# VectorE's up product directly behind the weighting, ahead of attention and routing, in a two-layer kernel

## What is computed

```python
q, k, v = ...                                  # three 128x128 projections of xn
attn = softmax(einsum('nqd,nkd->nqk', q, k) * HD ** -0.5)
x_att = (attn @ v) @ out_w.T + out_b           # 16 heads of 8; the 8 batches attend to each other at one sequence position

scores = sigmoid(xn @ w_gate.T)                # 16 experts in 4 groups: best 2 groups, best 4 experts
combine = normalised scores of the chosen experts, 0 elsewhere
g = silu(einsum('th,efh->tef', xn, w1_e));  u = einsum('th,efh->tef', xn, w3_e)
routed = einsum('tef,ehf,te->th', g * u, w2_e, combine)
shared = (silu(xn @ w1_s.T) * (xn @ w3_s.T)) @ w2_s.T
out = x + x_att + routed + shared
```

## Time and profile before

| | before |
|---|---|
| time, median of 3 runs | 355.44 us (355.14 to 356.28) |
| the profiled execution's own time | 355.92 us |
| its span, first to last instruction | 354.1 us |
| VectorE (DVE) busy | 311.0 us, 88% of the span |
| TensorE (PE) busy | 304.5 us, 86% |
| GpSimd (POOL) busy | 250.2 us, 71% |
| ScalarE (ACT) busy | 178.9 us, 51% |
| TensorE's granted clock, mean | 0.979 of full speed |

### The profile page before, as it was taken

How to read it: one execution, slowest core, us unless ns; L and a number is a source line. 1 busy time by engine, 2 the same in 40 slices (tenths; PEclk the granted TensorE clock), 3 DMA queues, 4 the chain that set the end, 5 groups by cost and what they waited for, 6 DMA issues and landing times.

```text
span 354.1 us, 5666 instructions
## 1 busy us (share of the span) xinstructions
PE 304.5 (86%) x1771; PEld 252.0 (71%) x1771; DVE 311.0 (88%) x826; ACT 178.9 (51%) x499; POOL 250.2 (71%) x162
## 2 busy tenths in 40 slices
PE   0568877899898987589999999899998999989995
PEld 0246555777686776477877887698987888878785
DVE  4995899979879677976999999899998999989795
ACT  3345766778786767677242531613516235162520
POOL 4184667826557361117999899989999899988671
PEclk9996999999999999879999999999999999999999
DMA  5590000000000000004853332423424334253102
GB/s 142 161 302 9 2 0 1 2 1 1 3 0 3 0 0 3 0 4 122 182 128 93 102 105 90 118 61 91 149 82 111 120 94 115 59 148 114 38 2 59
DMA packets 21321, 24.91 MB, mean 70 GB/s; under 512 B 2420, under 2 KB 12060, under 8 KB 21292
## 3 DMA queue, kind: packets, MB, share of 16 engines
q1 hardware_dynamic: 20248, 24.09, 24.7%
q10 hardware_dynamic: 820, 0.39, 0.4%
q0 software_dynamic: 224, 0.08, 0.1%
HBM read 22.19 MB, written 2.36 MB: 69 GB/s over the span
## 4 chain that ended last, share of the span: by engine, by line
DVE 37%; PE 34%; POOL 12%; issue 10%; ACT 6%; DMA 1%; DVEq 0%; POOLq 0%; ACTq 0%
PE Q L944 16%; PE VN L944 8%; PE T L944 7%; POOL prod_qk L874 6%; POOL prod_pv L884 4%; DVE hid L1632 4%; DVE rope_b L1368 3%; DVE rope_a L1366 3%; DVE att L1591 2%; PE T L940 2%; DVE sgc L1619 2%; DVE scr L1577 2%; DVE bst L1209 2%; DVE attn L1398 2%; DVE xT_lo L1419 1%
## 5 line engine op out<-in xcount | busy, mean ns | idle before, releaser
L874 POOL TENSOR_TENSOR prod_qk<-qkv 128x1024 f32<-128x1024 f32 x32 | 76.6, 2412 | 2.9 <-DVE above L1461 2.1
L884 POOL TENSOR_TENSOR prod_pv<-prob,qkv 128x1024 f32<-128x1024 f32 x32 | 69.0, 2195 | 7.4 <-DVE att L1591 5.1
L773 ACT ACTIVATE Q<-Q 128x512 f32<-128x512 f32 x48 | 27.5, 581 | 56.5 <-PE Q L944 56.3
L1632 DVE TENSOR_TENSOR hid<-T,sgc 128x512 f32<-128x512 f32 x64 | 43.4, 679 | 0.1
L944 PE MATMUL Q<-bias,ones 128*128 128x400 f32 (+1 forms) x64 | 30.3, 474 | 15.2 <-ACT v_ext L663 7.1
L1577 DVE TENSOR_REDUCE scr<-prod_qk 128x128 f32<-128x1024 f32 x32 | 38.8, 1211 | 5.0 <-POOL prod_qk L874 5.0
L944 PEld LDWEIGHTS Q<-w,hid 128*128 128x128 f32 x288 | 37.5, 191 | 3.4 <-DVE hid L1632 0.6
L944 PEld LDWEIGHTS VN<-w,hid 128*128 128x128 f32 x288 | 37.6, 191 | 3.1
L944 PE MATMUL Q<-w,hid 128*128 128x128 f32 x288 | 38.0, 275 | 0.4 <-DVE hid L1632 0.4
L944 PE MATMUL T<-xT_hi,w_hi 128*128 128x512 f32 x72 | 31.2, 434 | 8.2 <-DVE hid L1632 7.9
L1591 DVE TENSOR_REDUCE att<-prod_pv 128x128 f32<-128x1024 f32 x32 | 38.2, 1195 | 0.0
(11 more groups left out here) (186 smaller groups left out, 801.1 us busy)
## 6 DMA issues: line engine op xcount, KB each, us to landing
cw<-comb_table SPq DMA_DIRECT2D x62, 256.0 KB, 4.6
out_x<-fin SPq DMA_DIRECT2D x7, 256.0 KB, 4.5
x<-in_x SPq DMA_DIRECT2D x2, 256.0 KB, 3.1
wraw<-in_w1T SPq DMA_DIRECT2D x1, 512.0 KB, 4.2
w3raw<-in_w3T SPq DMA_DIRECT2D x1, 512.0 KB, 4.9
w<-in_w2T SPq DMA_DIRECT2D x1, 512.0 KB, 5.9
cw<-comb_table SPq DMA_DIRECT2D x4, 128.0 KB, 3.1
rope_s<-in_c_sin ACTq DMA_DIRECT2D x1, 256.0 KB, 5.1
```

The source lines that it names most:

```text
L773: act.activation(gated[:, :], gate_bank(n, s)[:, :], ACT.Silu).then_inc(sg_ready, 1)
L874: pool.tensor_tensor(prod_qk[:, t % 2], bc(qkv2[:, TH * half + t, j, 0:D], 1, NB), qkv2[:, :, j, D:2 * D], ALU.mult).then_inc(qk_prod, 1)
L884: pool.tensor_tensor(prod_pv[:, t % 2].rearrange("p (h e) b -> p b h e", e=HD), bc(prob[:, t].rearrange("p h b -> p b h"), 3, HD), qkv2[:, ...
L1632: V.tensor_tensor(hid[:, s % 3, :], UB[k][:, :], src, ALU.mult)\
```

## The change

`hidden` is called directly behind `weighted`, and attention and routing follow (in slices without weighting, `hidden` comes first). The score sums of units 3 and 5 take the late steps that only the last unit had. The sum of the exponentials goes to step 3 in all units (before 5, in the last unit 2), its inverse to step 4 behind the value sum (before 6, in the last unit 3). The last unit's exponential goes from step 1 to step 2, behind that slice's Silu. `biased` adds the bias for one slot instead of one batch; units 3 to 6 do that for the slot before, the last unit for the last two, and `residual` waits for its own slot alone.

```diff
@@ -781,7 +781,7 @@
                 if k < NSLICE:
                     gate(n, s)
                 for u, p in units(k):
-                    if p == (1 if u == END else 2):
+                    if p == 2:
                         exp_done(u)
                     if p == (8 if u == END else 9):
                         attT_evac(u)
@@ -842,11 +842,16 @@
                 settle(pool)
                 pool.tensor_tensor(x[:, c], x[:, c], l0_sum[:, :, :], ALU.add).then_inc(x1_ready, 1)
 
-            def biased(c):
-                if c == 0:
+            def biased(n):
+                j, half = place(n)
+                b = slice(TH * half, TH * half + TH)
+                if n == 0:
                     pool.wait_ge(ld_w2, 64)
-                pool.wait_ge(xn2_ready, 2 * c + 2)
-                pool.tensor_tensor(x[:, c], x[:, c], bc(bout2[:, :], 1, NJ), ALU.add).then_inc(x_biased, 1)
+                    pool.wait_ge(xn2_ready, 2 * TH)
+                if n == TH:
+                    pool.wait_ge(xn2_ready, 2 * NB)
+                pool.tensor_tensor(x[:, b, j, :], x[:, b, j, :], bc(bout2[:, :], 1, TH), ALU.add)\
+                    .then_inc(x_biased, 1)
 
             def low_part(dst, src, hi, hi_ready, ready):
                 pool.wait_ge(hi_ready, 1)
@@ -920,14 +925,18 @@
                         product_qk(n + 1, t, *place(n + 1))
 
                 next_qk(0)
-                if n + 2 < NB:
-                    biased(n + 2)
+                if 3 <= n < END:
+                    biased(n - 1)
                 less_max(n)
                 next_qk(1)
                 products_pv(n, n % NJ)
                 next_qk(2)
                 next_qk(3)
+                if n == END:
+                    biased(END - 1)
                 normalise(n)
+                if n == END:
+                    biased(END)
 
             for n in range(NSLOT):
                 unit(n)
@@ -1636,7 +1645,7 @@
 
                 j, half = place(n)
                 dve.wait_ge(yback_ps, n + 1)
-                dve.wait_ge(x_biased, TH * half + TH)
+                dve.wait_ge(x_biased, n + 1)
                 dve.wait_ge(fin_free, n + 1)
                 parts = 2 if n == END else 1
                 for h in range(parts):
@@ -1646,17 +1655,18 @@
 
             def attention_of(u, p):
 
-                first = (-4, -3, -2, -1) if u == 0 else (-7, -6, -1, 0) if u == END else (-8, -7, -2, -1)
+                short = u > 0 and BASE[u] - BASE[u - 1] < NS
+                first = (-4, -3, -2, -1) if u == 0 else (-7, -6, -1, 0) if short else (-8, -7, -2, -1)
                 if p in first:
                     scores(u, first.index(p))
                 if p == 0:
                     row_max(u)
-                if p == (2 if u == END else 5):
+                if p == 3:
                     sum_of_p(u)
-                if p == (3 if u == END else 6):
-                    over_sum(u)
                 if 3 <= p < 3 + TH:
                     values(u, p - 3)
+                if p == 4:
+                    over_sum(u)
                 if p == (10 if u == END else 15 if u == END - 1 else 14):
                     residual(u)
 
@@ -1681,11 +1691,11 @@
                 n, s = divmod(k, NS)
                 if k < NSLICE:
                     weighted(n, s, side(n, s))
+                if k < NSLICE:
+                    hidden(n, s, side(n, s))
                 for u, p in units(k):
                     attention_of(u, p)
                 route_second(k)
-                if k < NSLICE:
-                    hidden(n, s, side(n, s))
                 if k == 0:
                     route_limits(1)
                     route_masked(1)
```

## The result

The changed kernel takes 360.57 us (median of 6 runs, 358.85 to 361.18), the kernel before 355.38 us in the same comparison: ratio 1.014, 95% interval 1.0122 to 1.0158, so 5.2 us slower. The forecast was 359.5 us, within 356.7 to 363.7. The profiled execution took 360.52 us, against 355.92 before, so its parts must sum to +4.6.

A forecast was written before the change was run, and what follows sets the result against it. To slice 64 the prediction took VectorE's work plus 5.9 us to set the time, then the last unit's chain. 6.7 - 4.1 = +2.6, plus 1.5, gave +4.1 us: 359.5 us, range 356.7 to 363.7.

The forecast's parts named there:

- The pairs: On VectorE, a hidden product directly behind its weighting costs 0.12 us more; 54 new pairs before slice 64 add 6.5 us.
- The third rival: Dependent pairs on VectorE cost nothing because something else hides it, so the kernel gets faster: -3.1 us, 352.3; chance 0.05.
- Waits that go: To slice 64, 4.1 of VectorE's 5.9 us to spare goes as later steps fill its waits; 1.8 stays.
- What costs nothing: Bias additions, the residual's wait, the exponentials' sum and inverse, and the hidden product's wait for the up product add no time.
- pairs and maxima: Before slice 64, 6.5 us for pairs plus 0.2 for row maxima directly behind score sums in units 3 and 5: 6.7.
- A sign that did not come: In the profile after, VectorE's idle time to slice 64 would be near 2 us instead of 5.9.
- The last unit, +1.5: Behind slice 64, Exp's load waits for unit 6's copy and the wait moves to slice 67, about 2.4 us: +1.5.
- Bias additions at no cost: GpSimd's eight bias additions, 1.29 us each, stay eight and fit where it idles or waits for VectorE.
- All waits stay: First rival: GpSimd's waits survive because late sums only push its chain back, 363.6 us; chance 0.11.
- No difference: Second rival: every wait goes and the exponential's load is placed ahead of the copy, 355.3 us; chance 0.10.
- TensorE sets the pace: Fourth rival: earlier hidden products remove TensorE's 7.9 us of waits for them, at most 347.5 us; chance 0.02.

The follow-up runs named there:

- v3_hid_first: v2_tail_bias with the hidden product again ahead of attention and routing, as in the changed kernel: 355.54 us, ratio 1.0004 to the kernel before.
- v2_tail_bias: v1_tail with bias additions of slots 2 to 4 in units 0 to 2 and the last unit's second score sum one slice later: 349.69 us, ratio 0.9842.
- u3_no_dep: Changed kernel, same order, but in slices 1 to 8 the hidden product reads a constant tile and does not wait for the weighting: 353.03 us.
- u10_fin_slice: Changed kernel with the residual of units 0 to 5 one slice earlier: 360.84 us, ratio 1.0157 to the kernel before.
- u9_copy_late: Changed kernel with ScalarE's copy of unit 6's transposes one step later, behind the Silu of slice 67: 360.66 us.
- v1_tail: Changed kernel with hidden product back behind attention and routing, unit 6's copy behind slice 67's Silu, last unit's exponential sum and inverse at steps 2 and 3: 352.11 us.

## Why the prediction was right, and where it was off

- **The pairs, 6.5 us before slice 64.** Right, and for the reason given. v3_hid_first against v2_tail_bias shows 0.118 us a pair, and u3_no_dep that the wait for the result makes it. The third rival, that a pair costs nothing, has fallen.
- **Waits that go, 4.1 of 5.9.** Nearly right. Of the 5.6 us of listed waits 3.6 went: both second sums, the first unit's and ScalarE's 0.59 at slice 34, as forecast. The waits kept for units 4, 6 and 7 were put at 0.3, 0.3 and 1.2 and measured 0.38, 0.54 and 1.09. The other 0.3 of the 5.9 was idle time, but no listed wait.
- **The step that failed: "What costs nothing".** The sum lacks a wait, the 1.06 at slice 41. So the stage lost 4.0 and not 2.6: pairs and maxima at 6.7, less 3.6, and 1.06 make 4.2, beside the measured 4.0. That step asked whether TensorE would wait for `hid` and took the residual as settled by its wait for the bias. It did not look at who waits for the residual. The residual kept its slice, and there the hidden product overtook it, so the down product of slots 2 to 4 came up against it, TensorE's clock fell behind two of the waits, and ScalarE's Silu came late. u10_fin_slice, with the residual a slice earlier, has none of the three. That removing this 1.06 gains nothing measurable was not foreseen either.
- **A sign that did not come.** VectorE's idle time to slice 64 was to be near 2 us instead of 5.9; it is 5.2 (169.51 less 164.31). Listed waits are 3.1 of that. The rest is mostly in the pairs: the hidden product starts 0.72 behind its weighting, whose record ends at 0.68, and 0.04 in some 55 pairs is 2.2 us. So a part of each pair's 0.12 is idle time in the profile, and the sign was wrong even where the sum was right.
- **The last unit, +1.5.** Right: 1.6. The wait moved from slice 66 to 67 and measured 2.33 against 2.4; slice 67's weighting came 8.24 behind slice 64's against 8.2; the load stood behind the copy. u9_copy_late bears out the chain. From Exp's load to the Silu it is 3.23 us (336.85 to 340.08), two loads of 1.28, the exponential's 0.63 and 0.04: the rows show no drain. The Trainium skill, "ScalarE: Activation LUTs", section "What ACT_TABLE_LOAD costs", has about 1.38 us of drain with each load; this trace differs.
- **Bias additions at no cost.** As the price of the change, right as far as the runs show: unit 7's second sum, behind unit 6's new addition, waits 1.09 us, and 1.21 before. But the additions that units 3 to 5 had before and kept were not free, and the forecast did not see what could be gained there. v1_tail, with the additions where the change put them, still waits 0.76, 0.20 and 1.14 us at the second score sums of units 4 to 6; v2_tail_bias, with those of units 3 to 5 moved to units 0 to 2, at none of these. (The 1.31 at unit 7 is the later score sum's to remove.)
- **The other rivals.** All waits stay, 363.6: 3.6 of 5.6 us went. No difference, 355.3: unit 7's wait and the one in the last unit are there, and the load is not ahead of the copy. TensorE sets the pace: 7.0 of its 7.9 us of waits for hidden products went, others came (for `fin` 4.6, for weightings 3.7), and the kernel was slower.

In the profiled executions the 1.0 us gained ahead of the stage hid most of the error of the sum: +4.1 forecast, +5.6 from the first hidden product on, +4.6 in all. That was luck, and the medians show the error more fully: they differ by 5.2, and the forecast was 1.1 too low.

## What to carry to other kernels

Two VectorE instructions of which the second reads the first want another between them, if there is an independent one: here that is worth 0.12 us a pair, 6 us in all. Before filling an engine's waits with a cost of its own, ask whether the engine that it waits for can be relieved; and when an instruction overtakes others, list who waits for each that is overtaken, not only for the one that moved.

## What the runs showed of the hardware that was not expected

- A weighting of 0.68 us lets an independent product start 0.60 after it (u3_no_dep), and one that reads it 0.72 after (the changed kernel). Where the weighting itself follows a reciprocal these are 0.55 and 0.66.
- Two waits of TensorE of about 2 us (2.29 and 1.83) were each followed by 4 us at a mean clock of 0.57 (214 to 218 and 262 to 266 us). At the end of u9_copy_late much the same busy time brought the fall in one execution and not in another, and the two differ by 1.65 us. A kernel whose last product follows idle time of TensorE may thus have two times.
